# First attention of a four-layer model: experts' weights asked for one transfer at a time, scatters in pairs, and the look-up's tables waited for at the third tile

## The chip, the cores and the metric

One core of a Trainium2 chip runs the kernel. The metric is the device time of one execution in microseconds (us). All arithmetic is in float32.

## The reference, cut to what matters

The model has four layers; each adds an attention and a feed-forward part to x, both computed from the normalised x. Only the first layer is touched. Here x is 2 x 512 x 256, there are 16 query heads of 16 channels and 8 experts of 512 hidden units, of which each token uses two.

```python
q = rms_norm(jnp.dot(x, q_kernel)); k = rms_norm(jnp.dot(x, k_kernel)); v = jnp.dot(x, v_kernel)
q = q * qcos + rotate_half(q) * qsin
k = k * kcos + rotate_half(k) * ksin
logits = jnp.einsum('btkgh,bskh->bkgts', q * scale, k)
encoded = jnp.einsum('bkgts,bskh->btkgh', jax.nn.softmax(logits, axis=-1), v)
attn = jnp.dot(encoded.reshape(B, T, N * H), out_kernel)
...
top_w, top_i = jax.lax.top_k(jax.nn.softmax(x @ router_w), 2)
expert_weights = jnp.einsum('tk,tke->te', top_w / top_w.sum(-1, keepdims=True), onehot(top_i))
g = jax.nn.silu(jnp.einsum('td,edf->etf', x, w1)) * jnp.einsum('td,edf->etf', x, v1)
out = jnp.einsum('etf,efd,te->td', g, w2, expert_weights)
```

The last layer's weights are looked up: `w = lut[idx]`, with 16 entries. Half of that look-up (8 entries) is already done in the first layer, beside its experts.

## The kernel before, in words

The first layer is `rope_and_experts`, one block of programs, one program for each engine, ordered by semaphores. On the trace it runs from about 23 to 370 us. It has two parts.

**Attention.** TensorE (PE) projects 16 tiles of q and k (L544), the engines turn them by the tables of sines (L873 to L886), and then 32 groups follow, four for each of 8 pairs of batch and head group. A group is four score matmuls (`scores`, L586), four exponentials on ACT (L765) and four mixing matmuls (`mix`, L597), each of which raises `probs_used` by one, so that `probs_used` is 4 after the first group and 128 after the last. After each fourth group DVE copies the result, takes reciprocals and multiplies (L901 to L907). The output projection is `put_out` (L609), once for each batch, and DVE adds it to x (`add_out`, L913).

**Experts.** The router gives each token two slots. POOL scatters the tokens' rows to the DRAM tensor `f_rows`, sorted by expert, with 16 indirect DMAs (L388, two for each of 8 token tiles); before, all are issued as soon as POOL's part of the turning is done. Then 23 tiles of 128 slots are computed. For tile i, PE transposes the rows (`turn_x`, L618), multiplies by w1 (`gate`, L623), and by w3 (`raise_`, L623 too), DVE multiplies the two (`gate` of the DVE program, L920), PE transposes that (`turn_gated`, L648) and multiplies by w2 (`down`, L660). PE's order is written out by hand: gate(i+1), turn_gated(i), raise_(i+1), turn_x(i+2), down(i). ACT copies out (L772, L779, L785, L792) and POOL adds the result into `f_sums` by a scatter-add (L842), which raises `landed`.

**The order on SP, which issues the plain DMAs.** An expert's weights are three transfers of 512 KB (L505), 12 KB for each partition. All of an expert's memory lies in an arena that the attention uses too: experts 0 to 3 lie on what the projections used, experts 4 and 5 and the start of 6 on `qk` (48 to 80 KB of the arena), the rest of 6 and expert 7 on `probs` (80 to 96 KB). Before, SP waits for the turning, then for `probs_used` of 8, 12, 16 and 20 groups and loads experts 0 to 3 one after each; waits for the scatters; loads the rows of the first four tiles (L511); waits for the last group and loads experts 4 to 7; waits for the output projection and loads the look-up's three tables (`look.load`, L164 to L166, the index being 2144 KB on the place of `heads`); then loads the rows of tile i when `landed` says that tile i - 4 is done. PE waits for expert i's weights at gate(i), for i up to 7.

**The look-up** is 32 units on DVE, each two instructions (`Look.unit`, L178 and L182). They are spread over the tiles behind the gates. Before the first tile's gate DVE waits for the tables:

```python
units = 0
dve.wait_ge(look.t_loaded, 3 * 16)
for i in range(TILES):
    gate(i)
    while units * TILES < look.units * (i + 1):
        look.unit(dve, units, units, units // 4)
```

Of the kernel before, what the change touches and what calls it, by code (L numbers as in the profile page):

```python
# [14 lines left out]
ACT = mybir.ActivationFunctionType  # L15
AX = mybir.AxisListType

P = 128
B, T, C = 2, 512, 256
N = B * T  # L20
KC = C // P
# [3 lines left out]
HG = P // HP  # L25
NG = NH // HG
# [118 lines left out]
E_ALL = 8  # L145
# [252 lines left out]
def rope_and_experts(nc, whole, ps, d, x, xn, ident, looked_up):  # L398
# [4 lines left out]
    with Stage(nc, "a0") as s:  # L403
        route = Routing(nc, s, whole, d, "f0", False)
        rows = route.rows
        FF = 512
        FT = FF // P
        XS = 4
# [3 lines left out]
        def at(name, shape, kb, dtype=F32):  # L412
            return nc.alloc_sbuf_tensor_at("a0_" + name, shape, dtype, offset=arena + int(kb * 1024))

        w = at("w", [P, E_ALL, E_ROW], 0)
# [3 lines left out]
        by_sin, by_cos = at("by_sin", [P, 2, T], 36), at("by_cos", [P, 2, T], 40)  # L419
        wv, turn, sums_of = at("wv", [P, KC, NG * HD], 44), at("turn", [P, P], 44.5), at("sums_of", [P, P], 128.5)  # L420
        rstd, squares = at("rstd", [P, 2 * B, T // P], 45), at("squares", [P, T], 45.5)
        qk = at("qk", [P, 2, B * NG, T], 48)
        probs = at("probs", [P, 8, T], 80)
        heads = at("heads", [P, B * NG, T], 96)
        mixed, recip = at("mixed", [P, 2, T], 112), at("recip", [P, 2, T], 116)
# [7 lines left out]
        look = Look(s, d, looked_up, 0, LUT // 2, lambda name, shape, dtype=F32: at(  # L433
            name, shape, {"index_in": 96, "term": 113, "table": 149.5, "entry": 149.625}[name], dtype))
# [26 lines left out]
        GROUPS = NI * ST  # L461
# [5 lines left out]
        OUT_BANK = (2, 3, 6, 7)  # L467
        H1, H3, GT, XT, Y = 0, 2, 4, 5, 6
        TILES = SLOT_TILES

        score_bank = [j for gr in range(NARROW) for j in range(HG)]
        score_bank += [n % 6 for n in range(HG * (GROUPS - NARROW))]
# [13 lines left out]
        with nc.Block() as block:  # L486

            @block.sync
            def _(sp):
                route.load_first(sp)  # L490
                sp.dma_start(wv[:, :, :], d["a0_wv"].rearrange("(k p) n -> p k n", p=P)).then_inc(q_loaded, 16)
                sp.dma_start(wq[:, :, :], d["a0_wq"].rearrange("(k p) n -> p k n", p=P)).then_inc(q_loaded, 16)
                sp.dma_start(wk[:, :, :], d["a0_wk"].rearrange("(k p) n -> p k n", p=P)).then_inc(k_loaded, 16)
                sp.dma_start(turn[:, :], d["turn"]).then_inc(k_loaded, 16)
                sp.dma_start(rope[:, :, :], d["rope"]).then_inc(k_loaded, 16)
                route.load_rest(sp)
                sp.dma_start(sums_of[:, :], d["sums_of"]).then_inc(o_loaded, 16)
                sp.dma_start(wo[:, :, :], d["a0_wo"].rearrange("(g p) n -> p g n", p=P)).then_inc(o_loaded, 16)
                route.fill(sp)
                Stage.clear_stale(sp)  # L500

                def load_expert(e):
                    for first, name, parts in ((0, "f0_w1", KC), (KC * FF, "f0_w3", KC), (2 * KC * FF, "f0_w2", FT)):
                        n = KC * FF // parts
                        sp.dma_start(w[:, e, first:first + KC * FF].rearrange("p (k n) -> p k n", n=n),  # L505
                                     d[name][e, :, :].rearrange("(k p) n -> p k n", p=P)).then_inc(w_loaded[e], 16)

                def load_rows(i):
                    if i >= XS:
                        sp.wait_ge(landed, 16 * (i - XS + 1))  # L510
                    sp.dma_start(xs[:, i % XS, :], route.rows[i * P:(i + 1) * P, :]).then_inc(xs_loaded[i % XS], 16)  # L511

                sp.wait_ge(roped, NT)
                for e in range(E_ALL // 2):
                    sp.wait_ge(probs_used, HG * (GROUPS // 4 + e * GROUPS // 8))
                    load_expert(e)
                sp.wait_ge(route.scattered, 16 * TOP * TT)
                for i in range(XS):
                    load_rows(i)
                sp.wait_ge(probs_used, HG * GROUPS)  # L520
                for e in range(E_ALL // 2, E_ALL):
                    load_expert(e)
                sp.wait_ge(out_ready, B * KC)
                look.load(sp)
                for i in range(XS, TILES):
                    load_rows(i)
                sp.wait_ge(landed, 16 * TILES)
                for b in range(B):
                    of = slice(b * TT // 2, (b + 1) * TT // 2)
                    sp.dma_start(total[:, of, :], route.sums[b * T:(b + 1) * T, :].rearrange(  # L530
                        "(t p) c -> p t c", p=P)).then_inc(total_loaded, 16)

            @block.tensor
            def _(pe):
# [33 lines left out]
                def swap(t):  # L568
                    kind, b, g = tile(t)
                    if t >= 2:  # L570
                        pe.wait_ge(sin_done, t - 1)
                    pe.wait_ge(raw_ready, t + 1)
                    pe.matmul(ps[:, SWAP_BANK + t % 2, :], turn[:, :], qk[:, kind, b * NG + g, :],
                              start=True, stop=True).then_inc(swapped, 1)

                def scores(gr):
                    i, st = gr // ST, gr % ST
                    if exps_before(gr):
                        pe.wait_ge(probs_ready, exps_before(gr))
                    if gr == NARROW:  # L580
                        pe.wait_ge(sin_done, NT)
                    if st == 0 and i % NG == 0:
                        pe.wait_ge(roped, NT // B * (i // NG + 1))
                    for j in range(HG):
                        rows = slice(j * HP, (j + 1) * HP)
                        pe.matmul(ps[:, score_bank[HG * gr + j], :], qk[rows, 1, i, st * P:(st + 1) * P],  # L586
                                  qk[rows, 0, i, :], start=True, stop=True).then_inc(score_ready, 1)

                def mix(gr):
                    i, st = gr // ST, gr % ST  # L590
# [148 lines left out]
            def _(act):  # L739
# [7 lines left out]
                for t in range(NT):  # L747
                    kind, b, g = tile(t)
                    act.wait_ge(proj_ready, t + 1)
                    act.activation(qk[:, kind, b * NG + g, :], ps[:, t % 3, :], ACT.Copy).then_inc(raw_ready, 1)  # L750
                    if t >= NG and g == 0:
                        act.wait_ge(summed, t // NG)
                    act.activation(square[:, g, :], ps[:, t % 3, :], ACT.Square).then_inc(sq_ready, 1)
                    if t < NG:
                        route.take_rows(act, ps, SWAP_BANK + t % 2, t)
                    if t == NG:
                        route.weigh(act, ps, ROUTE_BANK)
                    if t >= NG and g == 1:
                        take_std(t // NG - 1)
# [47 lines left out]
            def _(pool):  # L807
# [10 lines left out]
                def turn_by_cos(t):  # L818
                    kind, b, g = tile(t)
                    pool.wait_ge(turned_ready, 2 * (t // NG) + 1)  # L820
                    if t >= 2:
                        pool.wait_ge(roped, t - 1)
                    pool.tensor_tensor(by_cos[:, t % 2, :], qk[:, kind, b * NG + g, :],
                                       turned[:, 0, t // NG, :], ALU.mult).then_inc(cos_done, 1)

                add_squares(0)
# [7 lines left out]
                for t in range(2 * NG, 4 * NG):  # L834
                    turn_by_cos(t)
                for tt in range(TT):
                    route.scatter(pool, tt)
                for i in range(TILES):
                    pool.wait_ge(y_ready, i + 1)
# [7 lines left out]
            def _(dve):  # L847
# [28 lines left out]
                def turn_by_sin(t):  # L876
                    kind, b, g = tile(t)
                    dve.wait_ge(turned_ready, 2 * (t // NG) + 2)
                    dve.wait_ge(swapped, t + 1)
                    if t >= 2:  # L880
                        dve.wait_ge(roped, t - 1)
                    dve.tensor_tensor(by_sin[:, t % 2, :], ps[:, SWAP_BANK + t % 2, :],
                                      turned[:, 1, t // NG, :], ALU.mult).then_inc(sin_done, 1)
                    dve.wait_ge(sin_done, t + 1)
                    dve.wait_ge(cos_done, t + 1)
                    dve.tensor_tensor(qk[:, kind, b * NG + g, :], by_sin[:, t % 2, :], by_cos[:, t % 2, :],  # L886
                                      ALU.add).then_inc(roped, 1)

                take_rstd(0)
# [39 lines left out]
                for m in range(KC):  # L929
                    add_out(1, m)  # L930
                units = 0
                dve.wait_ge(look.t_loaded, 3 * 16)
                for i in range(TILES):
                    gate(i)
                    while units * TILES < look.units * (i + 1):
                        look.unit(dve, units, units, units // 4)
                        units += 1
                for b in range(B):
# [1958 lines left out]
```

## Time and profile before

| | us |
|---|---|
| median of 3 runs | 2146.27 |
| lowest and highest | 2141.48, 2150.42 |
| the profiled execution, its own time | 2136.11 |
| its span, first to last instruction | 2134.3 |
| PE busy | 1869.5 (88% of the span) |
| DVE, ACT, POOL busy | 1287.6, 992.2, 1070.7 |
| mean granted clock of PE, of full speed | 0.936 |

The profile is of one execution. Times are microseconds from its first instruction; a row of the timeline gives start, length, engine, line and operation, output and inputs, the number of instructions merged, and in square brackets how long the engine had been idle and what ended that. PEld is the loading of PE's stationary operand, SPq and POOLq are issues of DMAs. PE's granted clock has two levels, 2.4 GHz (1.00) and 1.2 GHz (0.50).

### The profile page before, as it was taken

Reading aid. Unit: us, or ns where it says so; the run is one execution under the profiler, and the core shown is the slowest. Engines: PE = TensorE matmul, PEld = TensorE weight load, DVE = VectorE, ACT = ScalarE, POOL = GpSimd, SP = SyncE. Lnnn points to the kernel's source line nnn. Section 1 sums busy time; section 2 is a strip of 40 time slices with the busy share of each in tenths; the row PEclk is TensorE's granted clock in tenths of the full one; section 3 lists DMA queues with packets and bytes.
Section 4 is the critical chain, followed back from the end, with each engine's and each line's share of the span. In section 5 each row is a group of like instructions: output and inputs, shape, how many; then the busy total and the mean of one; then the engine's idle time right before and its main releaser. Section 6 shows DMA issues by size and latency. Waiting matters only on the chain. (4 is left out here: it accounts for less than half of the span.)

```text
span 2134.3 us, 45868 instructions
## 1 busy us (share of the span) xinstructions
PE 1869.5 (88%) x16855; PEld 1201.9 (56%) x16855; DVE 1287.6 (60%) x2490; ACT 992.2 (46%) x2430; POOL 1070.7 (50%) x2252
## 2 busy tenths in 40 slices
PE   8799897867789875559999999999999999999888
PEld 5422564422233453337777777677777777777653
DVE  2553554685559522347777777777777777777421
ACT  2374232216211431336665666566656665566421
POOL 0530222221120302047888888788888888787710
PEclk7899998989889896779999999999999999999899
DMA  5034322100110433012222222222222222222200
GB/s 150 1 130 155 75 47 60 37 0 1 47 56 1 111 101 98 18 40 57 61 52 55 62 61 63 57 52 61 62 52 52 62 61 52 51 62 46 43 4 20
DMA packets 227356, 121.36 MB, mean 57 GB/s; under 512 B 141600, under 2 KB 206656, under 8 KB 226880
## 3 DMA queue, kind: packets, MB, share of 16 engines
q1 hardware_dynamic: 221520, 109.06, 20.1%
q0 software_dynamic: 5616, 9.38, 2.1%
q8 instruction: 137, 2.24, 0.4%
q14 instruction: 83, 0.68, 0.1%
HBM read 84.88 MB, written 36.68 MB: 57 GB/s over the span
## 5 line engine op out<-in xcount | busy, mean ns | idle before, releaser
L2507 POOL TENSOR_TENSOR a_z<-a_z,a_term 32x14 f32<-32x14 f32 (+6 forms) x896 | 344.1, 384 | 70.2
L2503 POOL TENSOR_TENSOR a_term<-a_z,a_l 32x14 f32<-32x14 f32 (+6 forms) x896 | 341.0, 381 | 70.3
L2054 PE MATMUL ps<-all_xn,a_w_qkv 128*128 128x512 f32 x512 | 248.8, 612 | 3.5 <-DVE a_at L2553 3.5
L2533 DVE SCALAR_TENSOR_TENSOR a_qkv<-a_raw,a_taps,a_qkv 128x1024 f32<-128x1024 f32 x192 | 246.9, 1286 | 6.2
L2064 PE MATMUL ps<-a_w_z,all_xn 128*128 128x256 f32 x512 | 125.3, 389 | 17.3 <-ACT a_zs L2330 17.3
L2253 PE MATMUL ps<-a_out_t,a_w_out 128*128 128x256 f32 x512 | 130.3, 398 | 1.9 <-ACT a_out_t L2405 1.7
L2054 PEld LDWEIGHTS ps<-all_xn,a_w_qkv 128*128 128x128 f32 x512 | 89.7, 194 | 74.8 <-issue 67.9
L2326 ACT ACTIVATE a_raw<-ps 128x512 f32<-128x512 f32 x128 | 76.6, 598 | 115.9 <-PE ps L2054 115.2
L842 POOL DMA_INDIRECT f_sums<-a_y,a_xs x23 | 36.0, 1567 | 184.6 <-ACT a_y L792 181.7
L2064 PEld LDWEIGHTS ps<-a_w_z,all_xn 128*128 128x128 f32 x512 | 95.4, 194 | 29.8 <-ACT a_zs L2330 17.7
L388 POOL DMA_INDIRECT f_rows<-a_row,a_slots x32 | 36.4, 1137 | 137.3 <-DVE a_of_tile L377 127.9
L2253 PEld LDWEIGHTS ps<-a_out_t,a_w_out 128*128 128x128 f32 x512 | 93.5, 192 | 17.7 <-ACT a_out_t L2405 2.3
L2612 DVE SCALAR_TENSOR_TENSOR a_xf<-ps,a_zs 128x512 f32<-128x512 f32 x64 | 44.1, 689 | 94.3 <-POOL a_xnorm L2485 60.9
L2562 DVE SCALAR_TENSOR_TENSOR a_v<-ps,a_gates,a_decay 128x128 f32<-128x128 f32 x256 | 71.6, 340 | 46.5 <-ACT a_decay L2349 46.5
L2390 ACT ACTIVATE a_v_new<-ps,a_gates 128x128 f32<-128x128 f32 x256 | 72.9, 367 | 46.7 <-PE ps L2203 46.7
L2497 POOL COPY a_z<-a_l 32x256 f32<-32x256 f32 x64 | 26.8, 419 | 132.6 <-DMA a_l<-a_v_dram 132.3
L623 PE MATMUL ps<-a_w,a_xt 128*128 x184 | 88.4, 603 | 0.6 <-ACT a_xt L772 0.6
L2547 DVE SCALAR_TENSOR_TENSOR a_low<-a_gc_rows,a_gates,a_floor 128x128 f32<-128x128 f32 x256 | 88.5, 404 | 0.0
L2479 POOL TENSOR_TENSOR a_rstd<-a_var,a_half 128x4 f32<-128x4 f32 x64 | 67.1, 1048 | 22.7 <-DVE a_var L2631 22.7
L765 ACT ACTIVATE a_probs<-ps 128x512 f32<-128x512 f32 x128 | 66.1, 602 | 23.8 <-PE ps L586 23.8
L2220 PE MATMUL ps<-a_v_new,a_at 128*128 128x128 f32 x512 | 75.8, 292 | 1.2 <-ACT a_v_new L2390 1.2
L2336 ACT ACTIVATE a_qkv<-a_qkv 128x1024 f32<-128x1024 f32 x64 | 67.4, 1053 | 18.1 <-DVE a_qkv L2533 17.7
(321 smaller groups left out, 4287.7 us busy)
## 6 DMA issues: line engine op xcount, KB each, us to landing
a_gc_rows<-a_g_dram SPq DMA_DIRECT2D x64, 256.0 KB, 4.8
a_v_dram<-a_v SPq DMA_DIRECT2D x64, 256.0 KB
a_w<-in_f_w SPq DMA_DIRECT2D x24, 512.0 KB, 7.1
a_w_qkv<-in_a_w SPq DMA_DIRECT2D x16, 512.0 KB, 3.8
a_t_dram<-a_z SPq DMA_DIRECT2D x512, 8.0 KB
a_xs<-f_rows SPq DMA_DIRECT2D x46, 130.0 KB, 2.2
a_w_z<-in_a_w SPq DMA_DIRECT2D x16, 256.0 KB, 2.9
a_w_out<-in_a_wo SPq DMA_DIRECT2D x16, 256.0 KB, 3.1
```

What stands on the lines that cost most here:

```text
L623: mm = pe.matmul(ps[:, bank + i % 2, :], xt[:, i % 2, k, :], w[:, bass.ds(e, 1), first + k * FF:first + (k + 1) * FF], start=k == 0, stop= ...
L2054: mm = pe.matmul(ps[:, to, :], w_qkv[:, k, mt * P:(mt + 1) * P], xn[:, k, b * T:(b + 1) * T], start=k == 0, stop=k == KC - 1)
L2064: mm = pe.matmul(ps[:, to, i * 256:(i + 1) * 256], xn[:, k, tt * P:(tt + 1) * P], w_z[:, k, :], start=k == 0, stop=k == KC - 1)
L2220: mm = pe.matmul(bank(BO)[:, r, :], at[:, w % 4, r, :], v_new[:, r, :], start=w % CH == 0 and r == 0, stop=r == PR - 1)
L2253: mm = pe.matmul(bank(BO)[:, B * m:B * (m + 1), :], w_out[:, v, m * P:(m + 1) * P], out_t[:, v::VPK, :], start=v == 0, stop=v == VPK - 1)
L2326: act.activation(raw[:, mt, b, TAPS - 1:], ps[:, of, :], ACT.Copy).then_inc(raw_ready, 1)
L2390: act.activation(v_new[:, r, :], bank(BR)[:, r, :], ACT.Copy, scale=gate(K_BETA, w, r)).then_inc(vnew_ready, 1)
L2503: pool.tensor_tensor(term[:, 0:j, j + 1:], z[:, 0:j, j:j + 1].broadcast_to([HP, j, n]), rows[:, j:j + 1, j + 1:].broadcast_to([HP, j, n]), ...
L2507: pool.tensor_tensor(z[:, 0:j, j + 1:], z[:, 0:j, j + 1:], term[:, 0:j, j + 1:], ALU.add).then_inc(sub_step, 1)
L2533: dve.scalar_tensor_tensor(to, rows, tap, to, ALU.mult, ALU.add).then_inc(conv_ready if j == TAPS - 1 else conv_step, 1)
L2547: dve.scalar_tensor_tensor(low[:, r, :], gc_rows[:, w % 2, r, :], gate(K_GC, w, r), floor[:, :], ALU.subtract, ALU.min).then_inc(low_ready, 1)
L2562: dve.scalar_tensor_tensor(v0[:, w % 3, r, :], bank(BK)[:, 2 * (r // VPK) + 1, :], gate(K_NBETA, w, r), decay[:, r, :], ALU.mult, ALU.mult ...
```

## The change

It puts q and k of one pair next to each other in `qk` (pair first, then kind), so that the memory of a pair is free once its four groups are done. SP then asks for the weights of experts 0 to 5 one 512 KB transfer at a time, one after each group from the ninth to the 26th; those of expert 6 after the last group; those of expert 7 among the rows' loads, one behind each of tiles 4, 5 and 6. POOL's scatters go in pairs, each after three more groups (4, 7, ... 25). DVE waits for the tables behind the gate of the third tile, and the 32 units are spread over the last 21 tiles.

```diff
-        qk = at("qk", [P, 2, B * NG, T], 48)
+        qk = at("qk", [P, B * NG, 2, T], 48)
...
+        EARLY = 6
+        LOOK_FROM = 2
...
-                def load_expert(e):
-                    for first, name, parts in ((0, "f0_w1", KC), (KC * FF, "f0_w3", KC), (2 * KC * FF, "f0_w2", FT)):
-                        n = KC * FF // parts
-                        sp.dma_start(w[:, e, first:first + KC * FF].rearrange("p (k n) -> p k n", n=n),
-                                     d[name][e, :, :].rearrange("(k p) n -> p k n", p=P)).then_inc(w_loaded[e], 16)
+                PARTS = ((0, "f0_w1", KC), (KC * FF, "f0_w3", KC), (2 * KC * FF, "f0_w2", FT))
+
+                def load_part(e, j):
+                    first, name, parts = PARTS[j]
+                    sp.dma_start(w[:, e, first:first + KC * FF].rearrange("p (k n) -> p k n", n=KC * FF // parts),
+                                 d[name][e, :, :].rearrange("(k p) n -> p k n", p=P)).then_inc(w_loaded[e], 16)
...
                 sp.wait_ge(roped, NT)
-                for e in range(E_ALL // 2):
-                    sp.wait_ge(probs_used, HG * (GROUPS // 4 + e * GROUPS // 8))
-                    load_expert(e)
+
+                for n in range(3 * EARLY):
+                    sp.wait_ge(probs_used, HG * (9 + n))
+                    load_part(n // 3, n % 3)
                 sp.wait_ge(route.scattered, 16 * TOP * TT)
                 for i in range(XS):
                     load_rows(i)
                 sp.wait_ge(probs_used, HG * GROUPS)
-                for e in range(E_ALL // 2, E_ALL):
-                    load_expert(e)
+                for j in range(3):
+                    load_part(EARLY, j)
                 sp.wait_ge(out_ready, B * KC)
                 look.load(sp)
                 for i in range(XS, TILES):
                     load_rows(i)
+                    if i < XS + 3:
+                        load_part(EARLY + 1, i - XS)
...
-                    pe.matmul(ps[:, SWAP_BANK + t % 2, :], turn[:, :], qk[:, kind, b * NG + g, :],
+                    pe.matmul(ps[:, SWAP_BANK + t % 2, :], turn[:, :], qk[:, b * NG + g, kind, :],
...
                 for tt in range(TT):
+                    pool.wait_ge(probs_used, HG * (4 + 3 * tt))
                     route.scatter(pool, tt)
...
                 units = 0
-                dve.wait_ge(look.t_loaded, 3 * 16)
                 for i in range(TILES):
                     gate(i)
-                    while units * TILES < look.units * (i + 1):
+                    if i == LOOK_FROM:
+                        dve.wait_ge(look.t_loaded, 3 * 16)
+                    while units * (TILES - LOOK_FROM) < look.units * (i + 1 - LOOK_FROM):
                         look.unit(dve, units, units, units // 4)
                         units += 1
```

The other places where `qk` is read or written (L586, L587, L750, L823, L886) change their order of indices in the same way.

## Rows read from the trace of the kernel before

**Rows 1.** The page: PE's granted clock in 40 slices, in tenths.

```profile
PEclk7899998989889896779999999999999999999899
```

**Rows 2.** Busy time by stretch (us; in brackets instructions), PE clock, DMA share, GB/s.

```profile
135.00:145.00 10.00, 9.52 (x71) 2.17 (x70) 4.74 (x3) 8.25 (x17) 2.09 (x3) 1.00 0.80 275
175.00:185.00 10.00, 9.52 (x68) 2.17 (x67) 4.74 (x3) 8.25 (x17) 0.00 (x0) 1.00 0.00 0
210.00:215.00 5.00, 3.68 (x9) 1.33 (x7) 0.69 (x1) 0.60 (x1) 0.00 (x0) 1.00 1.09 378
215.00:220.00 5.00, 0.00 (x0) 0.00 (x0) 0.00 (x0) 0.00 (x0) 0.00 (x0) 0.75 0.86 349
220.00:225.00 5.00, 2.47 (x6) 1.58 (x7) 3.18 (x4) 0.60 (x1) 0.00 (x0) 0.50 0.01 4
...
240.00:250.00 10.00, 10.00 (x38) 6.08 (x37) 4.55 (x5) 3.50 (x7) 3.11 (x2) 1.00 0.27 44
```

**Rows 3.** The timeline, 211 to 243 us: start, length, engine, line.

```profile
211.80 1.88 PE L623 MATMUL ps<-a_w,a_xt 128*128 x4
...
212.00 0.69 DVE L913 TENSOR_TENSOR all_x<-all_x,ps 128x512 f32<-128x512 f32 x1 [2.75 <-PE ps L609]
...
221.79 0.69 DVE L920 TENSOR_TENSOR a_gated<-a_act_h,ps 128x512 f32<-128x512 f32 x1 [9.10 <-DMA a_entry<-in_entry]
...
222.53 1.11 PE L648 MATMUL ps<-all_ident,a_gated 128*128 128x128 f32 x4 [8.85 <-DVE a_gated L920]
...
223.44 3.62 PE L623 MATMUL ps<-a_w,a_xt 128*128 x4
...
229.23 1.88 PE L623 MATMUL ps<-a_w,a_xt 128*128 x4
...
230.95 0.60 PE L648 MATMUL ps<-all_ident,a_gated 128*128 128x128 f32 x4
...
235.05 1.88 PE L623 MATMUL ps<-a_w,a_xt 128*128 x4
...
239.13 0.69 DVE L920 TENSOR_TENSOR a_gated<-a_act_h,ps 128x512 f32<-128x512 f32 x1 [1.01 <-PE ps L623]
...
242.59 0.60 PE L648 MATMUL ps<-all_ident,a_gated 128*128 128x128 f32 x4
```

**Rows 4.** SP's DMA issues in the layer.

```profile
195.33 11.01 SPq L505 DMA_DIRECT2D a_w<-in_f_w  x12
212.00 0.34 SPq L164 DMA_DIRECT2D a_index_in<-in_f_index  x1
...
212.86 0.43 SPq L166 DMA_DIRECT2D a_entry<-in_entry  x1
234.01 105.08 SPq L511 DMA_DIRECT2D a_xs<-f_rows  x19
```

**Rows 5.** DMA issues with median us to landing, whole span.

```profile
a_w<-in_f_w SPq DMA_DIRECT2D x24, 512.0 KB, 7.1
...
a_index_in<-in_f_index SPq DMA_DIRECT2D x1, 2144.0 KB, 7.7
f_index_in<-in_f_index SPq DMA_DIRECT2D x1, 2144.0 KB, 13.8
...
a_entry<-in_entry SPq DMA_DIRECT2D x1, 8.0 KB, 8.9
```

**Rows 6.** Issues of rows between 120 and 240 us; then the landings of L388.

```profile
a_xs<-f_rows SPq DMA_DIRECT2D x6, 130.0 KB, 5.3
...
DMA to landing us min/median/max: 2.4/2.7/3.8
```

**Rows 7.** POOL's timeline: the second scatter-add.

```profile
236.00 1.60 POOL L842 DMA_INDIRECT f_sums<-a_y,a_xs  x1 [4.20 <-ACT a_y L792]
```

**Rows 8.** The timeline: a late mix and the first tile's transpose.

```profile
170.64 1.07 PE L597 MATMUL ps<-a_probs,a_values 128*32 128x512 f32 x8
...
195.12 0.44 PE L618 MATMUL ps<-all_ident,a_xs 128*128 128x128 f32 x2
```

## Prediction before the run

> **What bounds the kernel now.** I read the page first. PE is the busiest engine (88% of the span), and its granted clock has slices of 5 to 9 tenths in the first half and hardly any behind [rows 1]. The change lies between about 95 and 370 us, so next comes the busy time in short stretches [rows 2]. In the attention, PE is busy 9.52 us of 10 and ACT 8.25, with 275 GB/s of transfers in flight, and exactly the same with none: the two engines pace each other, and transfers cost them nothing. In the experts' tiles PE is busy 10.00 of 10, so PE bounds them. Between the two stands a hole: from 215 to 220 us no engine does anything, while the DMA moves 349 GB/s. The timeline shows why [rows 3]. PE finishes gate(1) at 213.68 (211.80 + 1.88). DVE finishes the last addition of the attention at 212.69, and then sits until 221.79 (9.10 us, ended by the landing of a look-up table), because the wait for the tables stands ahead of the first gate. PE then sat idle for 8.85 us. That wait ends last here, and it is what I price.
>
> **The wait for the tables, removed from the first tile.** The gate of tile 0 needs only two PSUM and SBUF operands that are there before 213.7. Without the wait it runs on DVE from about 212.7 to 213.4. In the steady rhythm, PE starts turn_gated 1.72 us behind the start of the gate's matmuls (230.95 - 229.23) [rows 3], so here at 211.80 + 1.72 = 213.52; the gate is done just before. It started at 222.53: **9.0 us** gained.
>
> **The clock that the hole costs.** Behind the hole the raise of tile 1 took 3.62 us for four matmuls, against 1.88 for the same four later [rows 3], and the granted clock from 220 to 225 us is 0.50, the level of 1.2 GHz, after a stretch in which PE did nothing [rows 2]. From turn_gated(0) to the next gate are 229.23 - 222.53 = 6.70 us; in the rhythm it is 235.05 - 230.95 = 4.10. With no hole, PE works on without a break from 210 to 215 us, where the row has 1.00, and stays at 2.4 GHz: **2.6 us** gained. I take it whole. The bound below is nothing, should the clock fall all the same. Both terms together are the same as one subtraction: gates 1 and 2 are 229.23 - 211.80 = 17.43 us apart, and one tile takes 5.82 (235.05 - 229.23), which leaves 11.61. The Trainium skill (TensorE: Matmul & The Clock Gate, Part 1) says that how long a matmul stretch stays slow after idling varies from run to run of one kernel, with a phase that the kernel doesn't set. By that rule the second term is anything from nearly nothing to more than 2.6, and the sum 9 to 13 or so; no row here shows its spread, as there is one profile.
>
> **The wait at the third tile, added.** Behind it on DVE are the look-up's units and gate(3); PE's turn_gated(3) waits for that. DVE's gate starts 4.08 us behind the start of that tile's matmuls (239.13 - 235.05) and takes 0.69 [rows 3]. Tile 2's matmuls start at 211.80 + 5.82 = 217.62, so gate(2) runs from 221.7 to 222.4. The tables were asked for from 212.00 on; the entries, the last, at 212.86 [rows 4], and they landed 8.9 us later, at 221.8 [rows 5]. So they are there, by 0.6 us. And that was behind 12 weight transfers that SP had begun to issue at 195.33; three are left there now. The upper bound is the other loading of the same index, 13.8 us [rows 5]: landing at 225.8. A tile with two units leaves DVE idle for 1.01 us (the row at 239.13), so two units take 5.82 - 0.69 - 1.01 = 4.12, and would then end at 229.9, where gate(3) is due at 227.5: 2.4 late. PE picks a gate's result up 2.77 us after it ends (242.59 - 239.82) [rows 3], so PE would not notice; it would from a landing at 226.2 on. I take 0, upper bound 2 us.
>
> **The units, respread.** 32 units over 21 tiles: one or two for each, as before, with two consecutive doubles at the start. A double leaves 1.01 us, so nothing is passed on: 0.
>
> **Weights of experts 0 to 5.** 18 issues under the attention where there were 12. SP has nothing else then. They are 18 x 0.524 MB = 9.4 MB over the 17 groups from about 132 to 174 us, some 225 GB/s, under the 378 of the row at 210 us [rows 2]. The attention's cover is the pair of rows at 135 and 175 us: 275 GB/s or none, with the same busy times. 0; I allow 1 us either way.
>
> **Weights of expert 6 and 7.** Expert 6 is issued at 195.33, alone, and is wanted at gate(6) near 241. Expert 7's parts stand behind the rows of tiles 4 to 6, that is behind `landed` of 1, 2 and 3. The first landed when SP went on to the rows of tile 4, at 234.0 [rows 4], and so at 222.4 now; the third at 234.0. With the 7.1 us median of a weight transfer [rows 5] the last is there by 241.2, and gate(7) comes at 211.80 + 6 x 5.82 = 246.7. Slack 5.5 us: 0. What the parts meet are the scatter-adds: POOL starts the second at 236.00 [rows 7], 2.0 us behind the landing of the first, so a landing may be that much later. A part is 1.4 us of the DMA at 378 GB/s. It fits; bound 3 x 1.4 = 4 us if it doesn't.
>
> **Scatters in pairs.** The 16 issues leave POOL's first free moments and go to 8 places; POOL has nothing else. The last pair goes after 25 groups, at 170.64 + 1.07 = 171.7 [rows 8], is issued by about 174 and lands by 178, with the 3.8 us maximum [rows 6]. SP's 18th part is issued at 174, then it waits for the scatters and asks for the rows of four tiles: 5.3 us [rows 6] and 2 us of issue, so about 185. They are wanted at 195.12 [rows 8]. Slack 10 us: 0. The new layout of `qk` moves addresses only: 0.
>
> **The sum.** 9.0 + 2.6 = 11.6 us, and everything behind moves up by it. Against the profiled execution's own time that is 2136.11 - 11.6 = 2124.5. This execution lies 10.2 us under the median of the three runs and under all of them; the layer's stall isn't what tells them apart as far as I can see, so I subtract from the median: **2146.27 - 11.6 = 2134.7 us**, 0.54% less. Not counted are the clock's changes in the stages behind, which fall at other moments once all is shifted: one busy stretch at half clock cost 2.6 us above, so two or three more or fewer of them are +-5 us.
>
> **Rivals.**
> 1. *The clock gives nothing back, or part of the stall returns.* PE is idle for 2 us before the second output projection as before, and the throttle could fall later; or the tables' wait costs its 2 us and expert 7's parts some of their 4. Then the gain is 9.0 or as little as 5: 2137.3 to 2141. For it: the tables make it by 0.6 us only. Against: the margins behind them.
> 2. *The gain is eaten.* The wait at the third tile takes the first one's place: it would need tables that land 11.6 us behind the tolerated 226.2, at 238. Or the shifted stages behind lose it in clock, some four or five such stretches. Time 2143 to 2149. For it: slices with 7 and 8 in the page's clock row. Against: nothing is in the DMA's way any more.
> 3. *Slower: the rows of the first tiles come late.* Place: SP's wait for the scatters, which now end at 178 and not before 140, behind which SP has the four rows' loads, and PE's turn_x(0), which stands ahead of the last head's sums and of the second output projection. Price: one for one from 195.12 on. It decides from 195.1 + 11.6 = 206.7; for a loss that shows, 217. Two landings one after the other, of a scatter and of the rows, each as slow as the index's 13.8 [rows 5], give 174 + 27.6 = 201.6: a part of the gain, not a loss. I price it at rows by 220: 2146.3 + 25 - 11.6 = 2160. For it: scatters and weights now share the DMA for 18 transfers. The Trainium skill (SBUF — State Buffer, section on SBUF's two separate sides) adds that a DVE instruction of some kinds keeps GpSimd from writing a DMA's descriptors until it ends, and the attention has such DVE work; by that rule a scatter is later by one DVE instruction. Against: the scatters before ran beside DVE's multiplications and, the last of them, beside the first weights, and none of them took over 3.8 to land [rows 6].
> 4. *It doesn't do what it says:* gate(0) has another wait behind the tables', or PE another behind gate(0), of the same length. Nothing in the rows points to one, since PE went on 0.05 us after the gate; 2146.
>
> **How the numbers follow.** A measurement of this kernel can tell about 0.5% from no change, 10.7 us. My forecast has 0.75, rival 1 0.12, rival 2 0.07, rival 3 0.04, rival 4 0.02. Of the forecast's share, its 11.6 lies just beyond 10.7, and the three runs before are 9 us apart, so a median can move by 4: I count 0.52 of the 0.75 as faster, 0.23 as the same. Rivals 1, 2 and 4 (0.21) are within it but for 0.01 on the slow side. Faster 0.52, same 0.43, slower 0.05. The range: 11.6 + 10 below for clock and spread (2124), and above up to no change at all (2146), which leaves out rival 3, most of rivals 2 and 4, and a tenth of the spread.
>
> **What would show it.** Right: DVE's first gate starts at 212.7, with no DMA as releaser; PE goes from gate(1) to turn_gated(0) without idling, and four matmuls of L623 take 1.88 in tile 1; gates 1 and 2 are 5.82 apart; DVE's wait at the third tile is under 1 us; PE's clock is 1.00 from 207 on; the attention's 10 us stretches still have ACT 8.25; the rows' landing is before 190; gate(7) doesn't wait. Wrong: PE idle before turn_gated(3), L618 waiting at 195, a longer period than 5.82 in tiles 2 to 6, or a gain in this layer that the stages behind give back in clock.

## The result, and the profile after

| | before | changed |
|---|---|---|
| median of 4 runs, us | 2148.35 | 2117.59 |
| lowest and highest | 2141.48, 2152.11 | 2112.97, 2120.13 |
| profiled execution, its span | 2134.3 | 2116.3 |
| mean granted clock | 0.936 | 0.942 |

The ratio is 0.9864, 95% interval 0.9825 to 0.9902: faster by 29 us (the medians lie 30.8 apart), where 11.6 were forecast, and outside the range (2124 to 2146). Three later comparisons of the same kernel gave 0.9907, 0.9867 and 0.9869.

In the layer the profile is what was forecast. The timeline of the changed kernel, with the rows that answer to [rows 3]:

```profile
211.35 1.88 PE L629 MATMUL ps<-a_w,a_xt 128*128 x4
...
212.15 0.68 DVE L927 TENSOR_TENSOR a_gated<-a_act_h,ps 128x512 f32<-128x512 f32 x1
...
213.06 0.60 PE L654 MATMUL ps<-all_ident,a_gated 128*128 128x128 f32 x4
...
213.50 1.88 PE L629 MATMUL ps<-a_w,a_xt 128*128 x4
...
217.17 1.88 PE L629 MATMUL ps<-a_w,a_xt 128*128 x4
...
221.24 0.69 DVE L927 TENSOR_TENSOR a_gated<-a_act_h,ps 128x512 f32<-128x512 f32 x1 [5.13 <-PE ps L629]
...
221.85 0.83 DVE L178 TENSOR_SCALAR a_term<-a_index_in,a_entry,a_table 128x1072 f32<-128x1072 int32 x1
...
222.99 1.88 PE L629 MATMUL ps<-a_w,a_xt 128*128 x4
```

The attention ended 0.45 us earlier than in the first trace. DVE's first gate no longer has a DMA as releaser; PE goes from gate(1) to turn_gated(0) without idling; the raise of tile 1 takes 1.88; gates 1, 2 and 3 are 5.82 apart (211.35, 217.17, 222.99). Behind the third tile's gate (221.24) DVE goes on to the first unit (L178) at once: the wait put there costs nothing. The windows answer to [rows 2]:

```profile
135.00:145.00 10.00, 9.52 (x70) 2.17 (x66) 4.73 (x4) 8.27 (x16) 2.88 (x3) 1.00 0.75 242
...
215.00:220.00 5.00, 5.00 (x21) 3.27 (x20) 0.69 (x1) 1.78 (x4) 1.62 (x1) 1.00 0.74 300
220.00:225.00 5.00, 5.00 (x20) 3.08 (x19) 3.69 (x5) 1.13 (x4) 1.06 (x1) 1.00 0.63 111
```

The attention's stretch is as before with 242 GB/s in flight, and the hole at 215 us is full of work at 1.00. SP's issues answer to [rows 4]:

```profile
131.40 42.65 SPq L508 DMA_DIRECT2D a_w<-in_f_w  x18
177.07 1.77 SPq L514 DMA_DIRECT2D a_xs<-f_rows  x4
...
222.31 0.43 SPq L508 DMA_DIRECT2D a_w<-in_f_w  x1
```

The four rows' loads are asked for at 177, 18 us ahead of their use. The next rows are SP's first issues of the second layer's attention and of its feed-forward part (before, then changed):

```profile
370.43 0.37 SPq L962 DMA_DIRECT2D a_wq<-in_a_wq  x1
...
576.38 0.33 SPq L1710 DMA_DIRECT2D f_su_ug<-in_f_su_ug  x1
```

```profile
358.21 0.37 SPq L970 DMA_DIRECT2D a_wq<-in_a_wq  x1
...
562.33 0.33 SPq L1718 DMA_DIRECT2D f_su_ug<-in_f_su_ug  x1
```

The second layer begins 12.2 us earlier (11.6 and the 0.45), and its attention takes 204.1 us in place of 206.0. The two profiles are 18 us apart, of which 14 lie up to the second feed-forward part and the rest behind it. The ratio says 29: so more than half of the gain is not where I priced it, and much of it is not even in these two profiles.

### The profile page after: what moved, and what is told of

It reads as the page before. It is cut to its first block and busy times, and to the rows that moved or that the text cites. A ratio compares the mean times of both kernels' runs of the same rounds, so it can differ in the third digit from the quotient of the medians.

```text
span 2116.3 us, 45869 instructions
## 1 busy us (share of the span) xinstructions
PE 1863.6 (88%) x16855; PEld 1199.2 (57%) x16855; DVE 1287.5 (61%) x2490; ACT 993.4 (47%) x2430; POOL 1075.6 (51%) x2252
## 5 line engine op out<-in xcount | busy, mean ns | idle before, releaser
L2515 POOL TENSOR_TENSOR a_z<-a_z,a_term 32x14 f32<-32x14 f32 (+6 forms) x896 | 349.3, 390 | 70.2
L388 POOL DMA_INDIRECT f_rows<-a_row,a_slots x32 | 36.9, 1154 | 173.4 <-DVE a_of_tile L377 127.9
```

The lines of the kernel that those rows point to most:

```text
L2515: pool.tensor_tensor(z[:, 0:j, j + 1:], z[:, 0:j, j + 1:], term[:, 0:j, j + 1:], ALU.add).then_inc(sub_step, 1)
```

## The experiments

All ratios are to the kernel before, run beside each other; where the profile is spoken of, it is that run's.

**The kernel before again, the moved wait alone, the rest alone, the change again.** `wait_only` puts only the last hunk of the diff into the kernel before; `rest_only` takes only that hunk out of the changed kernel.

> The kernel before once more, nothing changed. Both theories: ratio 1.000. Theory A (the moved wait gives 11.6 us in the layer, and the other 6 of the profile's 18, and up to 18 of the median's 29, are changes of PE's clock in later stages that differ from run to run): the profile of this run differs from the first one in its later stages by several us, and its stages up to 370 us by under 1. Theory B (what the clock does behind is fixed by where the stages begin): the later stages repeat within 1 to 2 us, span 2134.

> The kernel before with the tables' wait and the units moved to the third tile alone; weights, scatters and layout as before. Theory A: the sums are loaded 11.6 us earlier than before (349.1 in place of 360.7) and the ratio is that of the whole change, 0.986 within the noise. Rival (the weights' and scatters' moves carry part of it): a tables' landing near 221.8 that holds DVE at the third tile, and a ratio clearly nearer to 1, such as 0.993.

> The changed kernel with the tables' wait and the units as before, ahead of the first tile. The hole stays, but the tables are loaded without the weights of experts 4, 5 and 7 in front of them. Theory A: the entries land within 1 us of 221.8, the layer ends as before, ratio 1.000 within 0.003. Rival (weights and scatters carry part of the gain): the tables land earlier by up to 4 us (index alone at 378 GB/s from 212), and the ratio is 0.994 to 0.998.

> The changed kernel once more. Both: ratio 0.986 again if the 29 us are of the kernel; nearer to 0.9945 (11.6 us) if the second half was the luck of four runs. Its profile shows by stage whether attention 2 and the last layer again come out 1.8 and 2.5 us shorter than in the first profile of the kernel before.

| | ratio | 95% | attention 2, us |
|---|---|---|---|
| null | 0.9990 | 0.9966 to 1.0014 | 212.4 |
| wait_only | 0.9920 | 0.9888 to 0.9953 | 204.0 |
| rest_only | 0.9985 | 0.9956 to 1.0014 | 211.1 |
| after_again | 0.9907 | 0.9874 to 0.9941 | 204.0 |

"Attention 2" is the time from SP's first issue of the second layer to its first of that layer's feed-forward part, in the profile. Here the moved wait alone is the whole change, within the noise, and the rest is nothing. 0.9907 is 20 us, not 29, and not 11.6. The two profiles with the hole have second attentions of 212.4 and 211.1 us, against 206.0 in the first trace: theory B, that the later stages repeat, fell, and the first trace was on the short side. `rest_only` has 3 weight transfers ahead of the tables in place of 12, and shows what the other nine had cost them:

```profile
218.32 0.69 DVE L927 TENSOR_TENSOR a_gated<-a_act_h,ps 128x512 f32<-128x512 f32 x1 [8.05 <-DMA a_entry<-in_entry]
```

8.05 us of waiting in place of 9.10.

**Shifting the later stages, filling the hole, keeping the clock up.** A memset on DVE, behind the first layer's last transposes and ahead of its last additions:

```diff
+                dve.wait_ge(look.summed, look.units + 1)
+                dve.wait_ge(total_psum, B * KC)
+                dve.memset(look.term[:, :, 0:830], 0.0)
```

(0:1072 in `before_late`). `filled` has the following ahead of turn_gated(0); `warm` has eleven of the same kind, into bank XT and with the last expert's weights, ahead of the waits for the sums:

```diff
+                        for _ in range(10):
+                            pe.matmul(ps[:, GT, :], ident[:, :], w[:, 0, 0:FF], start=True, stop=True)
```

> The changed kernel with 1.4 us of idle work for DVE (a memset) behind the last transposes of the first layer, so that everything behind starts 1.4 us later. Theory C (half of the gain lies in the second attention's clock, which falls or stays up by where that stage happens to begin): the second attention takes 206 to 212 us in place of 204.0, with a stretch at half clock some 72 us behind its start, and the whole is 3 to 10 us slower than the changed kernel. Theory D (the later stages gain for another reason, such as less work left over): 1.4 us slower, the second attention 204.0.

> The kernel before with 1.9 us of the same memset behind the first layer's last transposes. Theory C: the second attention takes about 204 us in place of the 206 to 212 of the three profiles with the hole, so the kernel is 2 to 8 us faster than before although it does more. Theory D: 1.9 us slower, the second attention as before.

> The kernel before with ten matmuls of no use, some 8.6 us, in the hole between gate(1) and turn_gated(0), into a bank that is free. The tables are awaited as before. The forecast's own split (9.0 us of waiting, 2.6 of clock): DVE's first gate still waits 9.1 us, the granted clock stays at 1.00 behind it, and gates 1 and 2 are 17.43 - 2.6 = 14.8 us apart in place of 17.4. If the clock is not what made the second term: still 17.4. For the whole, theory C says anything from -8 to 0 us, by what the shift of 2.6 does to the second attention.

> The changed kernel with eleven matmuls of no use (9.4 us) in PE's 11 us of idling ahead of the loading of the sums at the end of the first layer. If PE's activity alone sets its clock: the transposes behind it (16 in 3.65 us) and the next norm's matmuls (8 in 5.68 us) run at 1.00, the layer and the norm are 3 to 5 us shorter, and the whole is faster than the changed kernel by that, less or more what theory C makes of the shift. If the matmuls disturb something or the clock falls all the same: no gain.

`after_late`: 0.9926 (0.9899 to 0.9954), where the changed kernel's ratios in other comparisons are 0.9864 to 0.9907. Its memset took 1.44 us, and its second attention 213.5 us in place of 204.1. But it delayed more than 1.44 us. The additions on DVE, which had run beside the transposes (L740), now stand behind the memset:

```profile
348.99 3.43 PE L740 MATMUL ps<-all_ident,a_total 128*128 128x128 f32 x16 [11.02 <-DMA a_total<-f_sums]
...
352.91 1.44 DVE L948 MEMSET a_term<- 128x1660 f32 x1 [17.08 <-PE ps L740]
354.26 2.41 DVE L953 TENSOR_TENSOR all_x<-all_x,ps 128x512 f32<-128x512 f32 x4
...
356.97 0.37 SPq L973 DMA_DIRECT2D a_wq<-in_a_wq  x1
```

From the transposes' start to the second layer are 7.98 us here and 4.59 in the changed kernel (353.62 to 358.21), so the delay is 3.4 us. The windows of the second attention from 72 us behind its beginning, changed kernel and then `after_late`:

```profile
430.20:442.20 12.00, 9.28 (x56) 3.70 (x48) 11.13 (x19) 1.98 (x3) 2.53 (x2) 1.00 0.00 1
442.20:454.20 12.00, 7.36 (x50) 2.86 (x48) 10.62 (x19) 1.97 (x3) 2.53 (x2) 0.93 0.00 0
```

```profile
429.00:441.00 12.00, 9.89 (x44) 3.73 (x36) 8.51 (x15) 1.66 (x3) 1.59 (x2) 0.72 0.01 2
441.00:453.00 12.00, 9.61 (x40) 3.72 (x40) 8.65 (x15) 1.39 (x3) 1.56 (x2) 0.72 0.00 0
```

The same program runs at 1.00 and 0.93 in the one and at 0.72 in the other. So a delay of 3.4 us at the end of the first layer went with 9.4 us more in the next stage, as theory C has it, in one profile. What about the delay does it is not shown. It is not the moment alone: second attentions that began at 353.3, 366.2 (`scat_burst`) and 377.1 us (`look_first`) all took 203.9 to 204.0.

`before_late`: 1.0017 (0.9996 to 1.0037), second attention 211.2: the expected gain did not come. But it was no test of it. Its first layer took 361 us, 14 more than in the first trace, where a memset of 1.9 had been added; so the second attention began elsewhere than intended. In `filled`, too, the first layer took 357 us. The reason stands at 129 us, in the first attention, far ahead of both edits: a stretch of 5 to 10 us in which PE, ACT and DVE all wait while POOL goes on. I call it the stop; the next experiments are about it.

In `filled` (0.9975, 0.9951 to 1.0) the hole itself answers (of the last row's four matmuls the window shows two):

```profile
224.85 1.88 PE L623 MATMUL ps<-a_w,a_xt 128*128 x4
...
226.57 8.75 PE L724 MATMUL ps<-a_w,all_ident 128*128 128x512 f32 x20
...
234.25 0.69 DVE L923 TENSOR_TENSOR a_gated<-a_act_h,ps 128x512 f32<-128x512 f32 x1 [8.51 <-DMA a_entry<-in_entry]
...
235.59 1.88 PE L623 MATMUL ps<-a_w,a_xt 128*128 x4
...
239.26 1.02 PE L623 MATMUL ps<-a_w,a_xt 128*128 x2
```

DVE still waits 8.51 us, but PE works in it, the next raise takes 1.88, and gates 1 and 2 are 14.41 us apart and not 17.43. Of the 3.02 between, 0.6 is the shorter wait and 2.4 the clock: the second term of the sum was right.

`warm`: 0.9844 (0.9818 to 0.9870). The changed kernel's transposes, and then those of `warm`:

```profile
353.62 3.58 PE L740 MATMUL ps<-all_ident,a_total 128*128 128x128 f32 x16 [11.09 <-DMA a_total<-f_sums]
...
348.69 1.97 PE L742 MATMUL ps<-all_ident,a_total 128*128 128x128 f32 x16 [1.19 <-DMA a_total<-f_sums]
```

They took 1.97 us in place of 3.58, and the layer 332 us.

**The stop.** The profiles of `before_late` and `filled` had it, the earlier ones had not. `scat_burst` takes one line out of the changed kernel, so that the scatters are back to back again:

```diff
-                    pool.wait_ge(probs_used, HG * (4 + 3 * tt))
```

`wait_only_b` is `wait_only` once more; `burst_late` is the kernel before with `pool.wait_ge(probs_used, HG * 12)` ahead of its scatters; `look_first` is `wait_only` with LOOK_FROM = 0.

> The changed kernel with the scatters back to back again, as before. Two profiles so far, both of kernels whose 16 scatters go back to back, have a stop of all engines but POOL from about 129 to 137 us, with 10 us of half clock behind it, some 12 us together; three others with such scatters and all five with scatters in pairs have none. Theory E (the back-to-back scatters now and then stop the other engines, and the pairs end that): this kernel is 2 to 5 us slower than the changed one in the median and has some runs 10 us above it. Rival F (the stop comes of something else, and the scatters' move is worth nothing): ratio as the changed kernel, 0.990 within 0.002.

> The kernel before with the moved tables' wait alone, once more. Theory E: a spread to the slow side that the changed kernel doesn't have, a median 2 to 5 us above scatters in pairs, and with a chance of some 2 in 5 the stop at 129 us in its profile. Rival F: as the changed kernel. Theory C for both: the second attention takes 204.0 us if its beginning is not shifted by the stop.

> The kernel before with the 16 scatters back to back, but begun after the 12th group, about 138 us, and not at 117. Theory E: if this run has a stop, it lies inside the scatters' 20 us, towards their end, near 150 to 158 us, and not at 129. Rival F: if there is a stop, at 129 to 137 as before. Without a stop it says nothing. The rows of the first tiles still arrive by 190, so otherwise as before: 1.000 within 0.003.

> The kernel before with the tables awaited behind the first tile's gate in place of the third's. The forecast's slack (PE takes a gate's result 2.77 us after it ends): DVE waits from 213.4 to 221.8 (8.4 us), gate(1), due at 215.9, starts near 226 behind two units, PE stalls before turn_gated(1) by 226.6 - 219.3 = 7 us, so of the 9.0 only 2 are left: the sums are loaded 2 to 3 us earlier than before. If the place of the wait doesn't matter once the first gate is ahead of it: 11.6 earlier.

| | ratio | 95% | ACT idle in the stop, us |
|---|---|---|---|
| scat_burst | 0.9940 | 0.9914 to 0.9966 | 7.14 |
| wait_only_b | 0.9935 | 0.9914 to 0.9956 | 7.89 |
| burst_late | 1.0004 | 0.9984 to 1.0024 | 5.03 |
| look_first | 0.9975 | 0.9947 to 1.0004 | 5.27 |

All four have the stop. It follows the scatters: in `burst_late` they run from 139.96 to 160.23, and DVE and ACT, at their longest idling, show:

```profile
149.08 1.07 POOL L388 DMA_INDIRECT f_rows<-a_row,a_slots  x1 [0.30 <-issue]
...
158.40 0.69 DVE L902 COPY a_mixed<-ps 128x512 f32<-128x512 f32 x1 [9.08 <-remote]
159.10 0.60 ACT L765 ACTIVATE a_probs<-ps 128x512 f32<-128x512 f32 x1 [5.03 <-remote]
159.27 0.96 POOL L388 DMA_INDIRECT f_rows<-a_row,a_slots  x1 [0.30 <-issue]
```

In the seven profiles that have it, ACT's longest idling begins 12 to 14 us behind the first scatter, beside the tenth to twelfth, and ends about with the last: at 159 here and at 134 in `scat_burst`. (DVE idles 4.85 us at such a place without a stop.) Rival F's "at 129 as before" is out.

`look_first` tells of the slack at the new wait. The wait behind the first gate lasts 9.68 us, and PE stalls one tile later:

```profile
220.40 1.88 PE L624 MATMUL ps<-a_w,a_xt 128*128 x4
...
231.57 0.84 DVE L178 TENSOR_SCALAR a_term<-a_index_in,a_entry,a_table 128x1072 f32<-128x1072 int32 x1 [9.68 <-DMA a_entry<-in_entry]
...
236.43 1.12 PE L649 MATMUL ps<-all_ident,a_gated 128*128 128x128 f32 x4 [8.32 <-DVE a_gated L921]
...
241.92 1.88 PE L624 MATMUL ps<-a_w,a_xt 128*128 x4
```

Gates 1 and 3 are 21.52 us apart, against 23.25 before [rows 3] and 11.64 in the changed kernel: 1.7 of 11.6 us are gained, 2 to 3 were expected. Moving the wait behind the first gate is not enough; at the third tile it is free.

**Which part ends the stop.** `after_c` is the changed kernel, `scat_burst_b` is `scat_burst` once more, `pairs_only` is the kernel before with the scatters in pairs, and `burst8` the kernel before with them in two rows of eight, the second after the 16th group.

> The changed kernel, beside the three others on one chip. Theory E (back-to-back scatters stop the other engines on some occasions, at about the tenth of them, and not on others): where they stop them now, ratio 0.986 to 0.988 (11.6 us of the hole, 11 of the stop, some 5 of the second attention's clock); where not, 0.991. No stop in its profile.

> The changed kernel with the scatters back to back. Theory E: either a stop in its profile and 10 to 13 us slower than the changed kernel beside it, or no stop and within 2 us of it. Rival F (the scatters' move is worth nothing): within 2 us of it with a stop in the profile.

> The kernel before with the scatters in pairs and nothing else. Theory E: no stop; the hole of 9.1 us stays; where kernels with back-to-back scatters stop, 0.994 to 0.996, where not, 1.000. With the 0.9935 of the moved wait alone, this should make the changed kernel's ratio. Rival G (the weights' transfers, not the scatters, are what ends the stop): a stop in its profile.

> The kernel before with the scatters in two bursts of eight, the second behind the 16th group. In the profiles with a stop it begins 10 to 13 us after the first scatter, at the ninth or tenth, and ends with the last. If a number in a row is what counts, two bursts of eight have no stop, and the ratio is that of the pairs alone. If the time or their density counts, a short stop of 1 to 2 us at each burst's end.

| | ratio | 95% | layer 1, us | attention 2, us |
|---|---|---|---|---|
| after_c | 0.9867 | 0.9839 to 0.9895 | 332.9 | 204.0 |
| scat_burst_b | 0.9930 | 0.9904 to 0.9957 | 343.4 | 210.0 |
| pairs_only | 0.9960 | 0.9938 to 0.9983 | 345.4 | 212.7 |
| burst8 | 0.9961 | 0.9938 to 0.9984 | 350.3 | 205.8 |

The windows from 112 to 142 us, `scat_burst_b` and then the changed kernel beside it:

```profile
112.00:122.00 10.00, 8.98 (x54) 2.03 (x52) 4.32 (x6) 4.78 (x10) 7.67 (x9) 1.00 0.24 86
122.00:132.00 10.00, 2.22 (x20) 0.47 (x16) 3.10 (x2) 2.67 (x5) 7.56 (x9) 0.91 0.28 102
132.00:142.00 10.00, 7.82 (x34) 1.73 (x34) 0.69 (x1) 5.39 (x11) 0.69 (x1) 0.58 0.25 80
```

```profile
112.00:122.00 10.00, 8.95 (x54) 2.03 (x52) 5.43 (x6) 5.67 (x13) 2.36 (x3) 1.00 0.08 27
122.00:132.00 10.00, 9.53 (x66) 2.18 (x66) 4.73 (x4) 8.25 (x18) 4.11 (x4) 1.00 0.38 115
132.00:142.00 10.00, 9.53 (x66) 2.18 (x66) 4.73 (x4) 8.25 (x18) 1.92 (x2) 1.00 0.82 257
```

From 122 to 132 us PE is busy 2.22 us of 10 and ACT 2.67, with POOL at its scatters 7.56 and the DMA at 102 GB/s only; then the clock is at 0.58. The timeline of the same stretch:

```profile
124.63 1.07 PE L603 MATMUL ps<-a_probs,a_values 128*32 128x512 f32 x8
...
130.47 0.96 POOL L388 DMA_INDIRECT f_rows<-a_row,a_slots  x1 [0.30 <-issue]
130.90 0.60 ACT L771 ACTIVATE a_probs<-ps 128x512 f32<-128x512 f32 x1 [6.41 <-remote]
131.73 0.96 POOL L388 DMA_INDIRECT f_rows<-a_row,a_slots  x1 [0.30 <-issue]
...
132.99 2.09 PE L592 MATMUL ps<-a_qk 32*128 32x512 f32 x8 [7.29 <-issue]
...
135.35 0.69 DVE L907 COPY a_mixed<-ps 128x512 f32<-128x512 f32 x1 [10.21 <-remote]
```

PE, ACT and DVE idle for 7.3, 6.4 and 10.2 us ("remote": what released them isn't in the trace), PE's next eight matmuls take 2.09 us, where the same eight take 1.14 at 1.00, and POOL issues on every 1.26 us. With pairs there is nothing of it, and the medians are 16 us apart (2132.13 and 2116.01). `pairs_only` has no stop, so it's the scatters and not the weights' transfers. `burst8` has none beside its first eight scatters and a short one at its second eight (ACT 0.78 and 1.92 us): a shorter row shortens the stop, and the number alone doesn't decide. It isn't free either: its first layer took some 5 us more than that of `pairs_only`. The ratios are equal all the same, and in the profile its second attention is 6.8 us shorter, which no run ties to the scatters.

**Once more beside each other.**

> The changed kernel with eleven matmuls of no use ahead of the sums' loading, once more and beside the changed kernel. Its profile had the layer and the norm 3 us shorter (the transposes 1.97 us in place of 3.58) and the second attention 205.3 in place of 204.0: 1.5 to 3 us faster than the changed kernel, 2 ratios of 1000 apart at most, so perhaps not told from it. Against: the second attention may fall to 210 and more, then 4 us slower.

> The changed kernel beside it. Theory E and C: 0.987 where back-to-back scatters stop the kernel before, 0.991 where not; second attention 204.0 to 204.1 as in all four profiles of the changed kernel's timing.

`after_d` 0.9869 (0.9837 to 0.9900), second attention 203.7. `warm_b` 0.9849 (0.9821 to 0.9876), 205.4. The version with useless matmuls is 3.4 us faster in the median (2112.93 and 2116.30), and its layer is 1.2 us shorter. But the intervals overlap, and in its first comparison the changed kernel itself was not beside it: whether it beats the changed kernel stays open. It clearly beats the kernel before.

## Why the prediction was wrong

**What held.** The wait removed: forecast 9.0 and 2.6, together 11.6; from SP's first issue of the first layer to its first of the second are 346.9, 344.9, 345.2 and 345.4 us in the four profiles with the hole and without any stop, and 334.3, 334.7, 333.4, 332.9 and 334.2 in the five of `wait_only` and the changed kernel: 345.6 and 333.9 in the mean, 11.7 less. The third tile's wait: 0. The units, the weights of experts 0 to 7, the rows' loads: 0, each with the slack that was worked out. None of the four rivals happened. Two readings were wrong, and no number rests on them. The lowest digit of [rows 1] is 6, not 5. And rival 3 took DVE's work in the attention to be of the kinds that hold up GpSimd's descriptors: it is copies and reciprocals out of PSUM (L901, L905) and products of two tensors (L907), and the scatters issued one every 1.26 to 1.27 us beside them, beside a reciprocal of 3.36 us too.

**The step that failed first: "Scatters in pairs ... 0".** I priced what moved (SP's wait, the rows' landing) and took the cost of what was removed from one profile, in which 16 scatters in a row happen to disturb nobody. In 7 of 10 profiles of kernels with 16 in a row they stop the other engines: the first layers of `scat_burst` and `scat_burst_b` took 345.2 and 343.4 us, those of the changed kernel 334.7, 333.4, 332.9 and 334.2, so 10.5 us for the stop and the clock behind it. Between `wait_only_b` and `wait_only`, one kernel with and without a stop in its profile, it is 12.2. In none of 9 profiles with pairs is there one. It comes in groups: none in the first three profiles of kernels with such a row (before, `null`, `wait_only`), one in each of the seven later ones. The medians of all runs agree with that: `wait_only` had 2117.77 and, where its profile has a stop, 2129.73; the kernel before had 2138.69 in the comparison whose profiles have none (and where `rest_only`, with pairs, gained nothing), and 2143.80 to 2146.71 in the four later ones, while the changed kernel stayed at 2116.01 to 2117.59. The kernel before lay at 2148.35 in the first comparison, so there too its runs look like those with a stop.

The sign stood in the prediction: the profiled execution was 10.2 us under the median of the three runs, and I wrote that the layer's stall isn't what tells them apart and asked no further. The stop is about as large. The term had no upper bound in my text; "Slack 10 us: 0" is a bound on the rows' landing, not on what the old burst cost.

**The step that failed second: the clock behind, "+-5 us".** I took it to be symmetrical and added nothing for it. It was not: the second attention took 203.7 to 204.1 us in the four profiles of the changed kernel and the first of `wait_only`, and 205.8 to 212.7 in the eight of kernels with the wait at the first tile, 209.6 in the mean. That is 5 to 6 us in favour. With the wait at the third tile and a stop it was 203.9, 207.2 and 210.0, and `after_late` made 213.5 of it by a delay of 3.4 us. So the short second attention isn't a merit of the moved wait, which takes nothing away from that stage; that it came out so is luck, if repeatable luck.

**The sum as the runs have it.** 11.6 (hole and its clock) + 10.5 (stop) + 5.5 (second attention) = 27.6 us, against 28 to 29 by the ratios of 0.9864 to 0.9869 and 20 (0.9907) where the stop is absent (11.6 + 5.5 = 17.1; the interval is 13 to 27). That they meet so closely is in part luck, since the sum leaves out everything behind the second attention. It took 1547.8 to 1554.1 us in the five profiles named above and 1552.0 to 1564.4 in the eight: 5.8 less in the mean, with ranges that overlap and no cause that a run shows. With it and with 12.2 for the stop the sum would be 35. Whether the stop was there in the first comparison's other runs, on which 29 rests, can't be seen: its one profile of the kernel before has none, and its time of 2136.11 is the lowest of all its runs (the next is 2141.48). That agrees, and isn't shown.

**What stays open.** What the stop is. PE, ACT and DVE wait, with releasers outside the trace. The Trainium skill (SBUF — State Buffer, on SBUF's two separate sides) has DVE and GpSimd lock each other out of a shared pair of ports, and says that PE and ACT never wait for anyone there; here PE and ACT stop too. They don't stop because of DVE either: in the timeline above ACT and PE go on at 130.90 and 132.99, ahead of DVE's next instruction at 135.35. So that rule isn't it. Late transfers aren't seen either: from 118 to 136 us of `scat_burst_b` the DMA queues carry the scatters alone (624 packets, 1.73 MB), and nothing else, instructions or data, lands during it or at its end. And 16 scatters in a row aren't enough by themselves: each profile has a second such row in a later layer (727.59 to 751.71 us in `scat_burst_b`), and in none of the 20 does an engine idle for a releaser outside the trace beside it. Why the stop is absent on some occasions was not found; the chip it isn't, as the first two sets of experiments ran on the same one.

## What to carry to other kernels

A change that spreads or delays something may remove a cost that one profile doesn't show: before pricing it at nothing, ask for a second profile of the kernel before, or leave the range open on that side. Try a long row of indirect DMAs from POOL in pieces when it runs beside other work: pairs cost nothing here, eight in a row still some 5 us of the layer. Place a wait behind the first tiles that don't need it. And when a stall of 10 us goes, look at the clock of the stage behind before crediting or blaming the edit: measure with small delays, and count only what survives them. When a profiled execution lies 10 us under the median of the runs, find out what the others have that it hasn't.

## What the runs showed of the hardware that was not expected

- 16 indirect scatters of 130 KB each, issued one every 1.26 us, stopped PE, ACT and DVE for 5 to 10 us from the tenth to twelfth on, in 7 of 10 profiles, with POOL and the DMA (102 GB/s) going on; the same number in a later layer never did.
- With a delay of 3.4 us ahead of it, PE's granted clock in a stage of 204 us was 0.72 over 24 us, in place of 1.00 and 0.93, and the stage took 9.4 us more.
- Ten useless matmuls in a hole kept the clock at 1.00 and gave back 2.4 us of the 2.6 behind it; eleven ahead of 16 transposes took these from 3.58 to 1.97 us.
